# Relative-position attention on one core: halved relative-value products, a picks buffer per query tile, and the band moved in two trimmed transfers

## The chip, the cores and the metric

The kernel runs on one core of a Trainium2 chip. The metric is the device time of one execution in microseconds; the time before is the median of three runs. The core's engines are named as the profile names them: PE (TensorE, its weight loads apart as PEld), DVE (VectorE), ACT (ScalarE), POOL (GpSimd), and SP, which in this kernel only issues transfers and waits.

## What is computed

A two-layer network on 16 sequences of 256 tokens with 128 features. Layer 0 is a second-order linear attention and a top-2 mixture of small experts; layer 1 is an attention with relative positions beside a top-2 mixture of gated experts. The change lies in the attention of layer 1 alone:

```python
# b = 16, s = 256, H = 16 heads of hd = 8, R = 64, VOCAB = 2R + 1
dist = jnp.clip(idx[None, :] - idx[:, None], -R, R) + R
pe_k = rel_emb_k[dist]
pe_v = rel_emb_v[dist]
score = jnp.einsum('bhqd,bhkd->bhqk', q, k) + jnp.einsum('bhqd,qkd->bhqk', q, pe_k)
attn = jax.nn.softmax(score, axis=-1)
ctx = jnp.einsum('bhqk,bhkd->bhqd', attn, v) + jnp.einsum('bhqk,qkd->bhqd', attn, pe_v)
return ctx @ W_out + b_out
```

Here `q`, `k` and `v` come from one projection of the normalized input. The relative part of the scores depends on the distance, which is clipped at 64 on both sides, and so does the relative part of the values.

## The kernel before

The stage `attn1_stage` goes through 16 sequences, each in two query tiles of 128 rows (`it` 0 and 1), so 32 tiles (`s`). In a tile the 16 heads go in eight pairs (`hp` 0 to 7), called slots below. Every engine has its own instruction list, written by hand; waits on semaphores tie them together.

**PE**, in each slot: `key_scores` (L1416) for the pair, `rel_scores` (L1407) of the same pair for the next tile, `transposes` (L1426) of the attention two pairs back. For the tile before it has, spread over the slots, four groups of `rel_values` (L1451, slots 2 to 5), four groups of `weigh` (L1463, value products, slots 3 to 6) and `folds` (L1471, slot 7). The projection of queries and keys of a later sequence (`project_qk`, L1225) stands in slot 1 of tile 1, that of the values (`project_v`, L1400) in slot 7 of tile 0. Both write the PSUM tile `a1ps_p`, which is also the second buffer of `rel_values`.

**Relative values.** The transposed attention of 16 query rows times a table of relative values gives, for each row, all shifted sums; `pick_diagonal` on DVE (L1618) multiplies by a mask that keeps those of the row's own shift, and `folds` sums them up. A group of 16 rows (`ig`) that reaches both key tiles takes two tables, one for each half of the array's columns. A group that reaches only one key tile has one table; the other half of the columns is fed with a table of zeros. Of the four groups of a tile two are of that kind:

```python
if len(use) == 1:
    use.append((len(TABLES), use[0][1]))
```

**The band.** The relative scores of a tile are 192 numbers per query and head (`BAND`) that have to be shifted by one column per row. ACT copies them from PSUM to `a1Rt` (`keep_R`, L1542). SP sends them to a buffer in memory, `skew` (`send_band`, L1741), and fetches them back with a row pitch that is one short (`fetch_band`, L1750) into `a1Sb`, which DVE adds to the scores (`add_scores`, L1609). Each tile's band goes in four quarters `q`, two head pairs each: four sends and four fetches of 384 KB. ACT may write a quarter of `a1Rt` again when the fetch of the tile before has landed.

**SP's list** sets the order of all transfers (`step` of the sync block). It is, for tile 0 of a sequence, with the query stacks of the next sequence (`a1stk<-parts`, L1268, three transfers per `fill`):

```python
fill(0); send_band(s + 1, nit, 0); fetch_band(s, it, 3)
fill(1); send_band(s + 1, nit, 1); fetch_band(s + 1, nit, 0)
fill(2); send_band(s + 1, nit, 2); fetch_band(s + 1, nit, 1)
send_band(s + 1, nit, 3); fetch_band(s + 1, nit, 2)
```

For tile 1 `fill(0)` issues the key stack (L1278), the other two fills are empty, and `send_parts` (L1259), which writes the split queries and keys of the sequence after next to memory, stands after `fetch_band(s + 1, nit, 1)`. A fetch waits for its send to have landed, a send for ACT's copies, and `fill(0)` of tile 0 for the `parts` that were sent in the tile before.

**Start.** DVE clears `a1vx` (L1680) and the edges of `a1Sb` (L1681, L1682); SP's first send and POOL wait for that.

## Time and profile before

| | us |
|---|---|
| median of three runs (lowest, highest) | 1687.14 (1685.96, 1688.66) |
| span of the profiled execution | 1677.5 |
| what lies around the span (median less span) | 9.6 |
| PE busy | 1552.2 (93%) |
| DVE busy | 904.4 (54%) |
| ACT busy | 732.4 (44%) |
| POOL busy | 299.0 (18%) |

The profile is one execution, from its first to its last instruction. The profiled execution has no time of its own other than its span; the runs were timed without the profiler. Busy shares are averages over stages: layer 0 takes up to about 830 us, the experts of layer 1 to about 1100, and the stage of the change about 1102 to 1660. A stretch of the trace therefore says more than the page's first lines. Matmuls are pipelined, so what one costs is read from the start of the next, not from its own duration.

### The profile page before, as it was taken

To read this page: it belongs to the slowest core of one execution; us is meant where nothing else is said; L and a number is where in the kernel's file an instruction comes from. 1 tells how busy PE (TensorE), PEld (TensorE's weight loads), DVE (VectorE), ACT (ScalarE), POOL (GpSimd) and SP (SyncE) were. 2 spreads that over 40 slices of the span, in tenths; PEclk is the share of its full clock that TensorE was granted. 3 is DMA by queue.
4 is the path that set the end of the run, shared out by engine and by line. 5 is a ranking of instruction groups with operands and counts; after the bars stand their busy time and mean duration, and the time that the engine had idled before them with its cause. 6 is when DMAs were issued, how large, how long until landed. Compare 5 with 4: busy or idle time off the path is not lost. (4 is left out here: it accounts for less than half of the span.)

```text
span 1677.5 us, 38807 instructions
## 1 busy us (share of the span) xinstructions
PE 1552.2 (93%) x14424; PEld 1233.4 (74%) x14424; DVE 904.4 (54%) x3193; ACT 732.4 (44%) x1975; POOL 299.0 (18%) x376
## 2 busy tenths in 40 slices
PE   6899999999999999999599999959999999999996
PEld 5668888888888888888365656537777777777764
DVE  5336545454545454545322222237877777777774
ACT  2322222222222222222223232258888888888873
POOL 2010201111111101010430000003323332333232
PEclk9999999999999999999699999979999999999998
DMA  4009400000000000000243232258889998899886
GB/s 118 0 8 86 105 8 7 8 8 6 6 6 5 7 5 7 3 10 4 85 114 114 77 112 85 72 166 245 250 241 251 237 250 235 246 246 254 236 235 173
DMA packets 234032, 181.50 MB, mean 108 GB/s; under 512 B 82703, under 2 KB 223913, under 8 KB 233888
## 3 DMA queue, kind: packets, MB, share of 16 engines
q1 hardware_dynamic: 228514, 167.17, 37.1%
q0 software_dynamic: 5376, 12.44, 2.7%
q8 instruction: 89, 1.46, 0.4%
q14 instruction: 53, 0.43, 0.1%
HBM read 103.63 MB, written 75.78 MB: 107 GB/s over the span
## 5 line engine op out<-in xcount | busy, mean ns | idle before, releaser
L1547 ACT ACTIVATE a1Pm<-a1Pm,a1nmx 128x256 f32<-128x256 f32 x512 | 255.5, 504 | 0.4 <-DVE a1nmx L1609 0.3
L1609 DVE CUSTOM_DVE_ANT_0 a1Pm<-a1ps_S,a1Sb 128x256 f32<-128x256 f32 x512 | 196.1, 421 | 77.2 <-issue 75.5
L768 DVE TENSOR_TENSOR a0AT<-a0ps_AM,mask 128x384 f32<-128x384 f32 x256 | 125.5, 551 | 192.5 <-PE a0ps_AM L588 192.1
L773 DVE TENSOR_TENSOR a0MT<-a0ps_AM,mask 128x384 f32<-128x384 f32 x256 | 138.4, 555 | 88.2 <-PE a0ps_AM L609 85.1
L1542 ACT ACTIVATE a1Rt<-a1ps_R 128x384 f32<-128x384 f32 x264 | 128.6, 487 | 106.7 <-PE a1ps_R L1407 96.9
L1162 DVE TENSOR_TENSOR f1hid<-f1ge,f1ps_b 128x512 f32<-128x512 f32 x80 | 55.0, 688 | 192.1 <-PE f1ps_b L1095 182.4
L1426 PE MATMUL a1ps_T<-ident,a1Pm 128*128 128x128 f32 x1024 | 155.9, 275 | 0.0
L607 PE MATMUL a0ps_AM<-a0AT 128*128 128x256 f32 x512 | 152.9, 380 | 0.0
L572 PE MATMUL a0ps_qk<-xnT_all,a0w_in 128*128 (+1 forms) x512 | 138.3, 393 | 2.0 <-PEq L151 1.3
L715 ACT ACTIVATE a0qk<-a0ps_qk 128x512 f32<-128x512 f32 x128 | 76.4, 597 | 119.3 <-PE a0ps_qk L572 119.3
L1407 PE MATMUL a1ps_R<-rel_st,a1stk 72*128 72x192 bf16 x528 | 90.0, 253 | 35.5 <-ACT a1Rt L1542 13.2
L719 ACT ACTIVATE a0v<-a0ps_v 128x512 f32<-128x512 f32 x64 | 38.2, 597 | 191.0 <-PE a0ps_v L598 187.0
L1426 PEld LDWEIGHTS a1ps_T<-ident,a1Pm 128*128 128x128 f32 x1024 | 115.0, 142 | 0.4 <-issue 0.2
L723 ACT ACTIVATE a0oT<-a0ps_o 128x512 f32<-128x512 f32 x64 | 38.2, 597 | 170.2 <-PE a0ps_o L621 170.2
L608 PEld LDWEIGHTS a0ps_AM<-a0AT 128*128 128x128 f32 x512 | 97.3, 190 | 13.2
L1105 PE MATMUL f1ps_o<-f1wo,f1hid 128*128 128x128 f32 x768 | 90.0, 277 | 15.4 <-DVE f1hid L1162 15.4
L572 PEld LDWEIGHTS a0ps_qk<-xnT_all,a0w_in 128*128 128x128 f32 x512 | 87.1, 190 | 19.9 <-issue 12.1
L1105 PEld LDWEIGHTS f1ps_o<-f1wo,f1hid 128*128 128x128 f32 x768 | 87.0, 192 | 19.7 <-DVE f1hid L1162 11.9
L1416 PE MATMUL a1ps_S<-a1stk 72*128 72x256 bf16 x512 | 101.4, 280 | 0.0
L1093 PE MATMUL f1ps_a<-f1xT,f1w 128*128 128x512 f32 x192 | 100.0, 603 | 0.7 <-issue 0.7
L1547 ACT ACTIVATION_READ_ACCUMULATOR a1Pm<-a1Pm,a1nmx 128x1 f32 x512 | 99.6, 195 | 0.0
L609 PE MATMUL a0ps_AM<-a0AT 128*128 128x128 f32 x512 | 99.0, 275 | 0.0
(246 smaller groups left out, 2991.0 us busy)
## 6 DMA issues: line engine op xcount, KB each, us to landing
skew<-a1Rt SPq DMA_DIRECT2D x132, 384.0 KB, 5.4
a1Sb<-skew SPq DMA_DIRECT2D x131, 384.0 KB, 7.0
a1stk<-parts SPq DMA_DIRECT2D x153, 64.0 KB
a1stk<-parts SPq DMA_DIRECT2D x51, 192.0 KB
parts<-a1prt SPq DMA_DIRECT2D x18, 384.0 KB
f1w<-in_L_ffn_w_kernel SPq DMA_DIRECT2D x16, 344.0 KB
f1w<-in_L_ffn_w_kernel SPq DMA_DIRECT2D x16, 320.0 KB
f1wo<-in_L_ffn_wo_kernel SPq DMA_DIRECT2D x16, 320.0 KB
```

The source lines that it names most:

```text
L572: ins = nc.tensor.matmul(ps_qk[:, i, :], w_in[:, i, p * P:(p + 1) * P], xnT_all[:, bass.ds(b * T, T)], start=True, stop=True)
L607: nc.tensor.matmul(M[:, 0:T], S[:, 0:P], S[:, 0:T], start=True, stop=True)
L609: nc.tensor.matmul(M[:, T:HB], S[:, T:HB], S[:, T:HB], start=False, stop=True).then_inc(M_done, 1)
L768: nc.vector.tensor_tensor(AT[i][h][:, :], ps_AM[i][h][:, 0:HB], mask[:, :], ALU.mult).then_inc(A_ready, 1)
L773: nc.vector.tensor_tensor(MT[i][h][:, :], ps_AM[i][h][:, 0:HB], mask[:, :], ALU.mult).then_inc(M_ready, 1)
L1093: nc.tensor.matmul(ps_a[u % 2][:, :], w[i][:, u * P:(u + 1) * P], xT[i][:, :], start=True, stop=True).then_inc(a_done, 1)
L1105: ins = nc.tensor.matmul(ps_o[i][:, s, :], hid[:, c, s * P:(s + 1) * P], wo[i][:, c, :], start=(c == 0), stop=(c == HC - 1))
L1416: ins = nc.tensor.matmul(ps_S[hp % 2][:, n, :], stk[par][:, 0, h, it * P:(it + 1) * P], stk[par][:, 1, h, :], start=True, stop=True)
L1426: ins = nc.tensor.transpose(ps_T[k % 2][:, n, jt, :], Pm[:, place(2 * k + n), jt * P:(jt + 1) * P], ident[:, :])
L1542: nc.scalar.activation(Rt[:, hp, :, :], ps_R[:, :, :].rearrange("p n c -> p c n"), ACT.Copy).then_inc(sm["R_ready"], 1)
L1547: nc.scalar.activation(Pm[:, place(h), :], Pm[:, place(h), :], ACT.Exp, bias=nmx[it][:, h:h + 1], scale=-1.0, accum_out=den[it][:, h:h + 1 ...
L1609: nc.vector.tensor_tensor_reduce(out=Pm[:, place(h), :], in0=ps_S[hp % 2][:, n, :], in1=bias_of(it, hp, n), scale=-1.0, scalar=3.0e38, op0 ...
```

## The change

It has six parts.

1. A group of `rel_values` with one table no longer multiplies by zeros: its two 8-row halves go to the two halves of the array's columns, four products instead of eight. Groups are taken in the order `turns`: a two-table group, the two one-table groups, the other two-table group.
2. `pick_diagonal` follows that: for a one-table group two instructions, each on 64 partitions and half the columns. What they leave unwritten must be zero, so the picks have a buffer per query tile, `X[0]` and `X[1]`, which DVE clears at the start. The wait for the folds goes one tile further back.
3. The groups of `weigh` stand in slots 3, 4, 6, 6 instead of 3, 4, 5, 6.
4. `project_qk` and ACT's `keep_qk` stand in slot 1 of tile 0 instead of tile 1, with waits to match.
5. Each `send_band` and `fetch_band` is two transfers of 64 rows, one of them 128 columns wide and the other 192 (`halves`), and `a1Sb` has a region for each query tile. Semaphores of the band count 32 instead of 16.
6. ACT waits for the send of the band, not for its fetch, before it writes `a1Rt` again.

```diff
-        Sb = m.sb("a1Sb", [P, HP, 2 * REL + BAND, 2])
+        Sb = m.sb("a1Sb", [P, HP, T + BAND, 2])
-        X = m.sb("a1X", [P, H1, P])
+        X = [m.sb(f"a1X{i}", [P, H1, P]) for i in range(2)]
...
+        def turns(it):
+            one_tile = [k for k in range(4) if alone(it, k)]
+            two_tiles = [k for k in range(4) if not alone(it, k)]
+            return two_tiles[0], *one_tile, two_tiles[1]
...
                 def project_qk(n):
-                    pe.wait_ge(sm["v_ready"], up(n - 1))
-                    pe.wait_ge(sm["X_ready"], up((n - 2) * 8))
+                    pe.wait_ge(sm["v_ready"], up(n - 2))
+                    pe.wait_ge(sm["X_ready"], up(((n - 2) * 2 - 1) * 4))
...
-                        if len(use) == 1:
-                            use.append((len(TABLES), use[0][1]))
                         for w in range(2):
-                            at = ig * GI + w * GH1
-                            for half, (t, jt) in enumerate(use):
-                                c = (1 - w) * (P // 2)
+                            at, c = ig * GI + w * GH1, (1 - w) * (P // 2)
+                            uses = uses_of(it, ig)
+                            pieces = [(w, n, *uses[0])] if alone(it, k) else [(half, 2 * n + w, *use) for half, use in enumerate(uses)]
+                            for half, col, t, jt in pieces:
...
-                        if it == 1 and hp == 1:
+                        if it == 0 and hp == 1:
                             project_qk(r * 2 + par + 2)
...
-                            if 3 <= hp < 7:
-                                weigh(s - 1, prev_b, pit, hp - 3)
+                            for q, at in enumerate((3, 4, 6, 6)):
+                                if hp == at:
+                                    weigh(s - 1, prev_b, pit, q)
...
-                        act.wait_ge(skew_in[hp // PQ], s * 16)
+                        act.wait_ge(skew_out[hp // PQ], s * 32)
...
+                    if alone(it, k):
+                        for w in range(2):
+                            rows = slice(w * (P // 2), (w + 1) * (P // 2))
+                            ins = nc.vector.tensor_tensor(out[rows, w:4:2, :, :], got[rows, 0:2, :, :],
+                                                          bc(bc(pick[rows, :], 1, H1), 1, 2), ALU.mult)
...
-                nc.vector.memset(Sb[:, :, 0:REL, :], 0.0)
-                nc.vector.memset(Sb[:, :, REL + BAND:2 * REL + BAND, :], 0.0).then_inc(sm["cleared"], 1)
+                for i in range(2):
+                    nc.vector.memset(X[i][:, :, :], 0.0)
+                nc.vector.memset(Sb[:, :, P:P + BAND, :], 0.0).then_inc(sm["cleared"], 1)
...
+                def halves(it):
+                    near, far = slice(0, P // 2), slice(P // 2, P)
+                    return ((near, P // 2, P), (far, 0, BAND)) if it == 0 else ((near, 0, BAND), (far, 0, P))
...
                 def send_band(s, it, q):
-                    c0 = 0 if it == 0 else 2 * (P - 1)
-                    sp.dma_start(skew[it][:, ps, c0:c0 + 2 * BAND], Rt[:, ps, :, :].rearrange("p n c h -> p n (c h)")).then_inc(skew_out[q], 16)
+                    for rows, c, w in halves(it):
+                        to = 2 * (c + (0 if it == 0 else P - 1))
+                        sp.dma_start(skew[it][rows, ps, to:to + 2 * w], Rt[rows, ps, c:c + w, :].rearrange("p n c h -> p n (c h)")).then_inc(skew_out[q], 16)
...
                 def fetch_band(s, it, q):
-                    sp.wait_ge(skew_out[q], (s + 1) * 16)
+                    sp.wait_ge(skew_out[q], (s + 1) * 32)
...
+                    for rows, _, w in halves(it):
...
+                        sp.dma_start(Sb[rows, ps, to:to + w, :].rearrange("p n c h -> p n (c h)"),
+                                     bass.AP(flat.tensor, at, [[2 * (HP * PITCH - 1), P // 2], [2 * PITCH, PQ], [1, 2 * w]])).then_inc(skew_in[q], 16)
```

Three places show how the instructions move. On PE, tile 1 of the first sequence, from the third group of `rel_values` to the end of slot 6, before (`a1ps_X` and `a1ps_p` are the two buffers of that group, `a1ps_c` takes the value products, `a1ps_S`, `a1ps_R` and `a1ps_T` are the scores, relative scores and transposes of a slot):

```order
1319 L1451 MATMUL a1ps_X<-a1PT,tabs 64x128 x8
1320 L1463 MATMUL a1ps_c<-a1PT,a1vx 32x128 x8
1321 L1416 MATMUL a1ps_S<-a1stk 128x256 x2
1322 L1407 MATMUL a1ps_R<-rel_st,a1stk 128x192 x2
1323 L1426 MATMUL a1ps_T<-ident,a1Pm 128x128 x4
1324 L1451 MATMUL a1ps_p<-a1PT,tabs 64x128 x8
1325 L1463 MATMUL a1ps_c<-a1PT,a1vx 32x128 x8
1326 L1416 MATMUL a1ps_S<-a1stk 128x256 x2
1327 L1407 MATMUL a1ps_R<-rel_st,a1stk 128x192 x2
1328 L1426 MATMUL a1ps_T<-ident,a1Pm 128x128 x4
1329 L1463 MATMUL a1ps_c<-a1PT,a1vx 32x128 x8
```

The same slots in the changed kernel:

```order
1319 L1463 MATMUL a1ps_X<-a1PT,tabs 64x128 x4
1320 L1475 MATMUL a1ps_c<-a1PT,a1vx 32x128 x8
1321 L1430 MATMUL a1ps_S<-a1stk 128x256 x2
1322 L1421 MATMUL a1ps_R<-rel_st,a1stk 128x192 x2
1323 L1440 MATMUL a1ps_T<-ident,a1Pm 128x128 x4
1324 L1463 MATMUL a1ps_p<-a1PT,tabs 64x128 x8
1325 L1430 MATMUL a1ps_S<-a1stk 128x256 x2
1326 L1421 MATMUL a1ps_R<-rel_st,a1stk 128x192 x2
1327 L1440 MATMUL a1ps_T<-ident,a1Pm 128x128 x4
1328 L1475 MATMUL a1ps_c<-a1PT,a1vx 32x128 x16
```

The third group has four products instead of eight, and the value products of slot 5 have gone to slot 6, where there are now 16.

On SP, tile 0 of a sequence, from the first query stack to the third send, before (L1741 sends a quarter of the band, L1750 fetches one):

```order
159 L1268 DMA a1stk<-parts 8x16x256 x3
160 L1741 DMA skew<-a1Rt 128x2x384
161 L1750 DMA a1Sb<-skew 128x2x384
162 L1268 DMA a1stk<-parts 8x16x256 x3
163 L1741 DMA skew<-a1Rt 128x2x384
164 L1750 DMA a1Sb<-skew 128x2x384
165 L1268 DMA a1stk<-parts 8x16x256 x3
166 L1741 DMA skew<-a1Rt 128x2x384
```

The changed kernel at the second stack and what follows it (L1770 sends, L1783 fetches):

```order
176 L1268 DMA a1stk<-parts 8x16x256 x3
177 L1770 DMA skew<-a1Rt 64x2x384
178 L1770 DMA skew<-a1Rt 64x2x256
179 L1783 DMA a1Sb<-skew 64x2x384
180 L1783 DMA a1Sb<-skew 64x2x256
181 L1770 DMA skew<-a1Rt 64x2x384
182 L1770 DMA skew<-a1Rt 64x2x256
183 L1783 DMA a1Sb<-skew 64x2x384
184 L1783 DMA a1Sb<-skew 64x2x256
185 L1278 DMA a1stk<-parts 24x16x256 x3
```

The order of quarters and stacks is the same; each band transfer is two instructions, of 64 rows each.

On DVE, at the start of the stage, before (the last row belongs to the first slot):

```order
562 L1680 MEMSET a1vx 128x2048
563 L1681 MEMSET a1Sb 128x8x128
564 L1682 MEMSET a1Sb 128x8x128
565 L1606 MEMSET a1taker 1x1
566 L1609 ISA a1Pm,a1nmx<-a1ps_S,a1Sb 128x256
```

And in the changed kernel:

```order
562 L1701 MEMSET a1vx 128x2048
563 L1703 MEMSET a1X 128x2048 x2
564 L1704 MEMSET a1Sb 128x8x384
565 L1619 MEMSET a1taker 1x1
566 L1622 ISA a1Pm,a1nmx<-a1ps_S,a1Sb 128x256
```

Two clears of 2048 elements have come in, and that of the band is 3072 elements in one piece.

## Rows read from the trace of the kernel before

**Rows 1.** Windows, steady part: length, busy us (instructions) by engine, clock, DMA share, GB/s.

```profile
1250.00:1600.00 350.00, 334.69 (x4836) 262.83 (x4830) 269.10 (x1205) 289.79 (x959) 106.15 (x144) 1.00 0.89 244
```

**Rows 2.** Timeline of PE, one sequence: start, us, instruction, records, idle before and releaser.

```profile
1315.38 0.34 PE L1407 MATMUL a1ps_R<-rel_st,a1stk 72*128 72x192 bf16 x2 [0.67 <-ACT a1PT L1558]
...
1316.20 1.09 PE L1451 MATMUL a1ps_X<-a1PT,tabs 128*64 128x128 f32 x16
1317.23 0.39 PE L1416 MATMUL a1ps_S<-a1stk 72*128 72x256 bf16 x2
...
1331.43 1.13 PE L1225 MATMUL a1ps_p<-xnT_all,a1w_in 128*128 128x256 f32 x4 [0.59 <-DVE a1vx L1594]
```

**Rows 3.** Waits, 1108 to 1655 us: who, for whom, us in total, times, longest.

```profile
ACT a1Rt L1542 <- PE a1ps_R L1407: 87.5, 107, 2.8
...
PE a1ps_R L1407 <- DMA a1stk<-parts: 6.4, 6, 2.0
PE a1ps_p L1225 <- DVE a1vx L1594: 6.1, 10, 0.7
```

**Rows 4.** Timeline of SP, one round from first query stack to the next.

```profile
1315.23 2.08 SPq L1268 DMA_DIRECT2D a1stk<-parts  x3
1317.36 0.45 SPq L1741 DMA_DIRECT2D skew<-a1Rt  x1
...
1321.18 0.47 SPq L1750 DMA_DIRECT2D a1Sb<-skew  x1
...
1324.35 0.46 SPq L1741 DMA_DIRECT2D skew<-a1Rt  x1
...
1329.90 0.36 SPq L1750 DMA_DIRECT2D a1Sb<-skew  x1
1330.30 1.38 SPq L1278 DMA_DIRECT2D a1stk<-parts  x3
1331.87 0.38 SPq L1741 DMA_DIRECT2D skew<-a1Rt  x1
...
1340.22 0.36 SPq L1750 DMA_DIRECT2D a1Sb<-skew  x1
...
1344.02 1.53 SPq L1259 DMA_DIRECT2D parts<-a1prt  x1
...
1348.21 1.38 SPq L1268 DMA_DIRECT2D a1stk<-parts  x2
```

**Rows 5.** Timeline of SP: the first query stack of the first and the last round.

```profile
1113.00 2.10 SPq L1268 DMA_DIRECT2D a1stk<-parts  x3
...
1620.89 2.08 SPq L1268 DMA_DIRECT2D a1stk<-parts  x3
```

**Rows 6.** Lines, 1108 to 1655 us: one of the picks; count, busy us, mean ns, idle before.

```profile
L1618 DVE TENSOR_TENSOR a1X<-a1ps_p,pick 128x512 f32<-128x512 f32 x62 | 42.5, 686 | 0.0
```

**Rows 7.** Timeline of DVE, start of the stage: clearing, and the first slot.

```profile
1102.58 1.76 DVE L1680 MEMSET a1vx<- 128x2048 f32 x1 [13.05 <-PEq L1031]
...
1115.69 0.06 DVE L1606 MEMSET a1taker<- 1x1 f32 x1 [9.20 <-DMA a1Sb<-skew]
```

**Rows 8.** Timeline of SP, start of the stage: the first four sends and three fetches.

```profile
1106.52 4.75 SPq L1741 DMA_DIRECT2D skew<-a1Rt  x4
1111.31 1.65 SPq L1750 DMA_DIRECT2D a1Sb<-skew  x3
```

**Rows 9.** The page's sixth part: band transfers, KB each, median us to landing.

```profile
skew<-a1Rt SPq DMA_DIRECT2D x132, 384.0 KB, 5.4
a1Sb<-skew SPq DMA_DIRECT2D x131, 384.0 KB, 7.0
```

More of the change, by code:

```diff
@@ L1376, in bias_of, with uses_of, alone @@
         def bias_of(it, hp, n):
-            c0 = REL * (1 - it)
+            c0 = BAND * it
             return Sb[:, hp, c0:c0 + T, n]
+        def uses_of(it, ig):
+            return [(t, jt) for t, (i2, jt, g2) in enumerate(TABLES) if (i2, g2) == (it, ig)]
+        def alone(it, k):
+            return len(uses_of(it, 2 * k)) == 1
+        def turns(it):
+            one_tile = [k for k in range(4) if alone(it, k)]
+            two_tiles = [k for k in range(4) if not alone(it, k)]
+            return two_tiles[0], *one_tile, two_tiles[1]
         def tiles_behind(r, i):
@@ L1427, in transposes, with rel_values @@
                     ins.then_inc(sm["T_done"], 1)
-                def rel_values(s, b, it, k):
-                    pe.wait_ge(sm["X_ready"], up(s * 4 + k - 1))
-                    if k == 1:
+                def rel_values(s, b, it, j):
+                    k, to = turns(it)[j], ps_X[j % 2]
+                    pe.wait_ge(sm["X_ready"], up(s * 4 + j - 1))
+                    if j == 1:
                         pe.wait_ge(sm["v_ready"], b + 1)
-                        pe.wait_ge(sm["qk_ready"], b + 3)
-                    if k == 0:
+                        pe.wait_ge(sm["qk_ready"], min(b + (3 if it == 0 else 4), B + 2))
+                    if j == 0:
                         pe.wait_ge(sm["Ta_ready"], (s + 1) * 4)
@@ L1464, in weigh, with folds @@
                                              start=(q == 0 and part == 0), stop=False)
-                def folds(s):
+                def folds(s, it):
                     pe.wait_ge(sm["X_ready"], (s + 1) * 4)
@@ L1531, in _ @@
                     weigh(last, B - 1, 1, q)
-                folds(last)
+                folds(last, 1)
                 project_out(last)
@@ L1574, in step @@
                             keep_rdT(s - 1)
-                        if it == 1 and hp == 1:
+                        if it == 0 and hp == 1:
                             keep_qk(nc, act, front, ps_p, bias_q, bias_k, r * 2 + par + 2)
@@ L1611, in add_scores, with pick_diagonal @@
                                                        accum_out=nmx[it][:, h:h + 1]).then_inc(sm["S_ready"], 1)
-                def pick_diagonal(s, k):
-                    v.wait_ge(sm["X_done"], s * 4 + k + 1)
-                    v.wait_ge(sm["c_done"], s)
-                    out = X[:, :, k * 2 * GI:(k + 1) * 2 * GI].rearrange("p h (n i) -> p n h i", n=4)
-                    nc.vector.tensor_tensor(out, ps_X[k % 2], bc(bc(pick[:, :], 1, H1), 1, 4), ALU.mult).then_inc(sm["X_ready"], 1)
+                def pick_diagonal(s, it, j):
+                    k, got = turns(it)[j], ps_X[j % 2]
+                    v.wait_ge(sm["X_done"], s * 4 + j + 1)
+                    v.wait_ge(sm["c_done"], up(s - 1))
+                    out = X[it][:, :, k * 2 * GI:(k + 1) * 2 * GI].rearrange("p h (m i) -> p m h i", m=4)
+                    if alone(it, k):
[3 more added lines that the diff above has]
+                                                          bc(bc(pick[rows, :], 1, H1), 1, 2), ALU.mult)
+                    else:
+                        ins = nc.vector.tensor_tensor(out, got, bc(bc(pick[:, :], 1, H1), 1, 4), ALU.mult)
+                    ins.then_inc(sm["X_ready"], 1)
                 def divide(s):
@@ L1689, in _ @@
                 for k in range(4):
-                    pick_diagonal(last, k)
+                    pick_diagonal(last, 1, k)
                 combine(last - 1)
@@ L1795, in _ @@
                 for q in range(QUARTERS - 1):
[L1796 to L1797 removed]
+                    sp.wait_ge(skew_in[q], (2 * B + 1) * 32)
+                sp.wait_ge(skew_out[3], (2 * B + 1) * 32)
 def store_stage(nc, x_all, out):
```

21 lines of the change are left out of this document (9 added, 12 removed).

## The prediction

> **What bounds the kernel now.** I began with the page's forty slices, took from them the stretch of the second attention (about 1102 to 1660 us), and put its steady part into one window [rows 1]. There PE is busy 334.69 of 350 us (96%), ACT 83%, DVE 77%, the DMA engines 0.89, and the granted clock is 1.00 throughout (2.4 GHz). So matmul work taken out of this stage should come out of the time, unless something that is nearly as late takes over. The timeline of PE [rows 2] shows how small its holes are: two of 0.6 us in a batch element. The waits of the whole stage [rows 3] say who makes them: the value bias on DVE (the query projection shares a PSUM tile with it), and the query stacks, a DMA that SP issues. ACT by contrast waits 87.5 us for PE in 107 places, so it has room.
>
> The second thing to see is SP's own order [rows 4]. One batch element (two query tiles) is one round of SP: three query stacks with sends and fetches of the band between them, the key stack, more sends and fetches, then `parts` for the element after next, and the next round's first stack may not go before these parts have landed. The round is therefore a closed loop of issues and landings: 1315.23 to 1348.21 is 32.98 us. From the first to the last first-stack [rows 5] there are 15 rounds in 507.89 us, 33.86 each. That PE does wait for the query stacks, 6.4 us in six places, says that this loop arrives just in time with PE at 96%: **two bounds of nearly the same length**. What PE saves counts only as far as SP's round shortens too.
>
> **The change part by part.** *Halved products.* A group of 16 records (8 products) starts at 1316.20 and the next matmul at 1317.23: 1.03 us [rows 2]. Of four groups per tile two lose half: 1.03 us less per tile, 33 us over 32 tiles, 2.06 us per element, all of it on PE. Records still alternate between the column halves, so I take half the number as half the time. If the two halves no longer overlapped, nothing would be saved (0); there is no way to save more than half. I take the half, since a group with two tables already alternates in the same way at that rate.
>
> *The moved query projection.* In tile 0 the PSUM tile is free, so the wait of 0.59 us goes [rows 2] (6.1 us in ten places over the stage [rows 3]). The ACT wait of 0.67 us that PE has in the tile without a projection turns up in tile 1 instead. About 0.4 us per element is gained. *The moved value products* (3, 4, 6, 6) are the same instructions in the slots that the picks left emptier; nothing.
>
> *Picks.* One pick is 686 ns [rows 6]. Two half-length ones cost between 0.69 and 1.37 us together; at the upper end DVE gets 1.4 us more per tile. DVE is at 77%, and a pick is not used before the folds of slot 7, so this is hidden. It would cost if DVE fell behind PE by a slot; it has 0.77 x 16.9 = 13.0 us of work per tile, 14.4 after. *Two pick buffers* take away a wait that no row shows; nothing.
>
> *ACT's wait on the send instead of the fetch* frees the band tile sooner. What ACT waits for is PE, in 107 places [rows 3], so nothing is gained in the steady part.
>
> *Start of the stage.* DVE clears 2048 elements in 1.76 us from 1102.58, and the first band send leaves SP at 1106.52 when it is done with all clearing [rows 7, 8]. The change clears twice 2048 more and 3072 instead of 2048: 3 x 1.76 + 2.64 + gaps of 0.16 puts the end at about 1111.0. The four sends so far waited for ACT's copies and were out at 1111.3; now eight go from 1111.1 at about 0.42 us each, to 1114.4. The first fetch, issued at 1111.31 and waited for until 1115.69, comes 3.1 us later and its second half 0.4 more: **+3.5 us**, bare, since DVE is idle 9.2 us there. Bounds: 0 if the copies still set the pace, 4.5 if all of it shows.
>
> *The halved transfers.* Every send and fetch of 384 KB [rows 9] becomes one of 128 KB and one of 192 KB: a sixth fewer bytes, twice the issues. An issue holds SP 0.36 to 0.47 us [rows 4]; 16 more per element are 6 to 7 us of SP. Not all lies on the loop. I walk the round of [rows 4] with 0 at 1315.23:
> - To the third send, 9.12 us, is pure issuing. Four second halves before it: 10.9.
> - That send's landing releases the fetch at 14.67, 5.55 later. If the queue ahead decides, it lands at 14.67 as before; if the issue decides, at 10.9 + 0.45 + 5.55 = 16.9. The queue ahead is as long in packets and shorter in bytes. I take 15.4.
> - The key stack follows 0.85 later instead of 0.40: 16.25 (was 15.07).
> - From the keys to the landing of the next send it is 9.92 us (24.99), most of it the keys' own transfer; the second half hides under it. Half of the sixth that the bands lose, 8%, comes off: 25.4.
> - From there to `parts` it was 3.80 us, with waits for ACT and for a send that ACT had released late. These are over by then, and three issues with their halves remain: 2.6, so 28.0 (was 28.79).
> - The parts landed 4.19 later; less 8%: **31.9 instead of 32.98, -1.0 us per round.**
>
> Low bound: nothing of the second halves shows and the landings shrink by the full sixth; the round is then shorter than PE's own and PE sets it, 33.86 - 2.06 - 0.4 = 31.4, or -2.4. High bound: the issue decides and no landing shrinks: 16.9, keys 17.75, 27.7, 30.3, 34.5, or +1.5. I take -1.0 because at a DMA share of 0.89 a landing is mostly queue, and the queue is what shrinks.
>
> For the halves the trace of before has no example. A rule speaks against them: the Trainium skill, page DMA: Bandwidth & Descriptors, section Rules for kernel authors, says of two transfers to disjoint partition halves "Don't bother — they serialize", and wants one transfer over all partitions. By it alone the sum would keep the issues and lose the shrinking, which is the high bound above; by the bytes of the rows it is the -1.0. No run so far shows which.
>
> **The sum.** 15 rounds x -1.0 = -15.0; start +3.5; the last two tiles, after the last stack, are PE's and SP has nothing left to do in them, -2.0. Together -13.5 us. The profiled span is 1677.5 us and the median of the runs 1687.14, 9.6 more around the span, which the change doesn't touch: 1664 in the profile, **1674 us** by the runs.
>
> **The rivals.**
> - *PE sets the pace alone.* For it: 96% busy, waits for the stacks only 6.4 us in total. Against: with 2.4 us less per element the loop would have to come down from 33.9 to 31.4 with 16 more issues in it. 15 x -2.4 + 3.5 - 2 = -34.5: 1653 us.
> - *SP's issues set the pace.* The second half of each transfer holds the stacks behind it; the round goes to 34.5, PE waits for the query stacks at the start of every second tile, and what the products save turns into that wait. This decides from the point where the third send lands more than about 1.2 us later than now. 15 x 1.5 + 3.5 - 2 = +24: 1711 us; half-way there, +0.7 per round, 1699. For it: the pure issuing up to the third send. This is where the rule of the Trainium skill cited above would lead.
> - *Nothing in the end.* Rounds at -0.1 to -0.3 pay for the start: 1684 to 1690 us.
> - *The products don't overlap.* If the halves of the array took turns instead of working side by side, PE would keep its time and the rounds theirs; this falls together with the case before.
>
> **How the numbers follow.** The sum's case, rounds shorter by 0.3 to 2.0 us (1665 to 1684), gets 0.45; PE alone (1650 to 1665) 0.22; nothing 0.13; SP's issues (1691 to 1711) 0.20. What a measurement of this kernel can tell from no change is about 0.2%, 3.4 us. So faster 0.67, same 0.13, slower 0.20. The range leaves out the lower tip of the second case and the upper half of the last: 1652 to 1700 us.
>
> **What would show it.** Right: the rounds between first stacks come to 32.9 us on average; PE's busy time falls by about 33 us and its share in the steady window to 93 or 94%; PE's wait for the query stacks grows from 6.4 to 15 or 20 us; the landing of the key-phase send comes 9 us after the keys; DVE's first pass waits about 3.5 us longer. If the rounds are 31.4 and the waits for stacks are gone, PE was the only bound and I gave the loop too much weight. If they are 34 or more, with issues back to back on SP and PE waiting 2 us or more for the stacks in each element, the second halves lay on the loop. If the groups of 8 records last 1 us, the products didn't overlap. A landing that is longer than before at fewer bytes would be against every case here.

## The result and the profile after

The changed kernel takes **1713.57 us** (median of four runs, 1711.48 to 1717.45), the kernel before 1686.55 beside it: ratio 1.0174, 95% interval 1.0148 to 1.0201. It is slower by 27 us (forecast: 1674, range to 1700). The profiled execution is the slowest of the four and spans 1715.7 us.

The steady window, as in [rows 1] (length; PE, PEld, DVE, ACT and POOL busy; clock; DMA share; GB/s):

```profile
1250.00:1600.00 350.00, 310.55 (x4267) 242.46 (x4261) 265.92 (x1172) 274.78 (x907) 98.50 (x135) 0.96 0.79 201
```

Every engine does less in the same 350 us, and the DMA engines are down from 0.89 to 0.79. Nothing that the window counts as busy looks like the bound. What it does not count is SP's issuing. Timeline of SP, one round, the counterpart of [rows 4] (at 37.78 us the longest of 15; their mean is 35.64):

```profile
1371.27 2.13 SPq L1268 DMA_DIRECT2D a1stk<-parts  x3
1373.44 1.46 SPq L1770 DMA_DIRECT2D skew<-a1Rt  x2
1374.95 1.27 SPq L1783 DMA_DIRECT2D a1Sb<-skew  x2
1376.26 2.12 SPq L1268 DMA_DIRECT2D a1stk<-parts  x3
1378.42 1.27 SPq L1770 DMA_DIRECT2D skew<-a1Rt  x2
1379.73 2.25 SPq L1783 DMA_DIRECT2D a1Sb<-skew  x2
1382.03 2.12 SPq L1268 DMA_DIRECT2D a1stk<-parts  x3
1384.19 1.27 SPq L1770 DMA_DIRECT2D skew<-a1Rt  x2
1385.50 1.27 SPq L1783 DMA_DIRECT2D a1Sb<-skew  x2
1386.81 1.26 SPq L1770 DMA_DIRECT2D skew<-a1Rt  x2
1388.12 1.28 SPq L1783 DMA_DIRECT2D a1Sb<-skew  x2
1389.44 1.52 SPq L1278 DMA_DIRECT2D a1stk<-parts  x3
...
1394.58 1.27 SPq L1770 DMA_DIRECT2D skew<-a1Rt  x2
1401.08 1.24 SPq L1783 DMA_DIRECT2D a1Sb<-skew  x2
...
1405.05 0.53 SPq L1259 DMA_DIRECT2D parts<-a1prt  x1
...
1409.05 2.12 SPq L1268 DMA_DIRECT2D a1stk<-parts  x3
```

From 1371.27 to 1391 each row begins where the one above it ended: tile 0 of the list has become pure issuing. One real wait is left, 5.2 us from 1395.85 to 1401.08, for the landing of a send. Over 15 rounds SP issues for 30.5 us of 35.6 on average; in the kernel before it was 16.0 of 33.9. A pair of halves holds SP for 1.27 us, where one transfer of 128 rows took 0.36 to 0.47 [rows 4]. Band lines of both kernels (ns, minimum/median/maximum), first after, then before:

```profile
L1770 SPq DMA_DIRECT2D skew<-a1Rt x264: 589/612/1737, 1113.4 to 1691.6; - x132
L1783 SPq DMA_DIRECT2D a1Sb<-skew x262: 592/609/1926, 1118.7 to 1692.9; - x131
```

```profile
L1741 SPq DMA_DIRECT2D skew<-a1Rt x132: 359/382/1487, 1106.5 to 1651.6; - x132
L1750 SPq DMA_DIRECT2D a1Sb<-skew x131: 359/366/1732, 1111.3 to 1652.0; - x131
```

A transfer of 64 rows costs *more* to issue than one of 128 rows, at its minimum (0.59 against 0.36 us) as at its median. A round has eight sends and eight fetches by quarter, so SP issues 16 x (1.22 - 0.37) = 13.6 us more in a round of 34. Waits from 1108 to 1700 us, first the engines (as [rows 3]), then SP's own queue, after and before (before: 1108 to 1655 us; who, for whom, us, times, longest):

```profile
DVE a1taker L1619 <- DMA a1Sb<-skew: 38.4, 29, 9.5
PE a1ps_R L1421 <- DMA a1stk<-parts: 35.2, 15, 3.8
```

```profile
SPq L1783 <- DMA skew<-a1Rt: 58.3, 25, 5.2
SPq L1770 <- ACT a1Rt L1555: 13.8, 27, 1.2
```

```profile
SPq L1750 <- DMA skew<-a1Rt: 119.6, 69, 6.3
SPq L1741 <- ACT a1Rt L1542: 103.1, 66, 3.8
```

PE waits 2.3 us for the query stacks in each of 15 elements (35.2 us; 6.4 before [rows 3]), and SP waits for a third of what it did: in the kernel before 119.6 us for sends to land and 103.1 for ACT, now 58.3 and 13.8. The first share in the list of the chain that ended last is `SPq 13%` (before, `PE 21%`).

The transfers themselves did become shorter, as the sixth part of the profile's page has it (KB each, median us to landing; before, 5.4 and 7.0 [rows 9]):

```profile
skew<-a1Rt SPq DMA_DIRECT2D x132, 192.0 KB, 3.6
a1Sb<-skew SPq DMA_DIRECT2D x131, 192.0 KB, 4.2
skew<-a1Rt SPq DMA_DIRECT2D x132, 128.0 KB, 3.7
a1Sb<-skew SPq DMA_DIRECT2D x131, 128.0 KB, 4.6
```

And the start of the stage, DVE and then SP, as in [rows 7, 8]:

```profile
1104.09 1.76 DVE L1701 MEMSET a1vx<- 128x2048 f32 x1 [13.06 <-PEq L1031]
...
1110.72 2.62 DVE L1704 MEMSET a1Sb<- 128x3072 f32 x1 [0.59 <-issue]
1122.86 0.06 DVE L1619 MEMSET a1taker<- 1x1 f32 x1 [9.52 <-DMA a1Sb<-skew]
```

```profile
1113.37 5.29 SPq L1770 DMA_DIRECT2D skew<-a1Rt  x8
1118.71 3.88 SPq L1783 DMA_DIRECT2D a1Sb<-skew  x6
```

From the first clearing to the first slot it is 18.8 us, 13.1 before: +5.7.

### The profile page after: what moved, and what is told of

Read it like the earlier page. It is cut to its first block and busy times, and to the rows that moved or that the text cites. A ratio compares the mean times of both kernels' runs of the same rounds, so it can differ in the third digit from the quotient of the medians.

```text
span 1715.7 us, 38103 instructions
## 1 busy us (share of the span) xinstructions
PE 1544.1 (90%) x13904; PEld 1225.4 (71%) x13912; DVE 927.5 (54%) x3258; ACT 733.0 (43%) x1975; POOL 298.9 (17%) x376
## 5 line engine op out<-in xcount | busy, mean ns | idle before, releaser
L1440 PE MATMUL a1ps_T<-ident,a1Pm 128*128 128x128 f32 x1024 | 169.1, 291 | 0.3 <-ACT a1Pm L1560 0.3
L1421 PE MATMUL a1ps_R<-rel_st,a1stk 72*128 72x192 bf16 x528 | 94.9, 265 | 62.1 <-DMA a1stk<-parts 35.2
L1440 PEld LDWEIGHTS a1ps_T<-ident,a1Pm 128*128 128x128 f32 x1024 | 125.5, 152 | 1.1 <-ACT a1Pm L1560 0.6
L1421 PEld LDWEIGHTS a1ps_R<-rel_st,a1stk 72*128 72x128 bf16 x528 | 46.7, 102 | 90.1 <-DMA a1stk<-parts 39.4
L1430 PE MATMUL a1ps_S<-a1stk 72*128 72x256 bf16 x512 | 106.5, 292 | 4.0 <-DVE a1nmx L1622 4.0
```

The source lines that it names most:

```text
L1421: ins = nc.tensor.matmul(ps_R[:, n, :], stk[par][:, 0, 2 * hp + n, it * P:(it + 1) * P], rel_st[:, it, :], start=True, stop=True)
L1430: ins = nc.tensor.matmul(ps_S[hp % 2][:, n, :], stk[par][:, 0, h, it * P:(it + 1) * P], stk[par][:, 1, h, :], start=True, stop=True)
L1440: ins = nc.tensor.transpose(ps_T[k % 2][:, n, jt, :], Pm[:, place(2 * k + n), jt * P:(jt + 1) * P], ident[:, :])
```

## The experiments

The round below is the mean distance of POOL's copies of `a1xb`, one per element, between the second and the last (15 intervals); by this measure before has 33.64 us and the changed kernel 35.56. Ratios are to the kernel before, run on the same chip beside each group. "Move" is the query projection in tile 1 or tile 0; "parts" is where SP sends them. "Half" products come with the other parts of the change that the columns don't name (picks, slots of `weigh`, ACT's wait on the send). Not in the columns: e5, e7, e11, e12 and e16 clear the edges of the band first. The groups ran on different chips, so between groups the ratios compare better than the times, and each round is that of one profiled execution.

| run | products | transfers | move | parts | us | ratio (95%) | round |
|---|---|---|---|---|---|---|---|
| before | full | whole | tile 1 | late | 1686.55 | 1 | 33.64 |
| after | half | trimmed halves | tile 0 | late | 1713.57 | 1.0174 (1.0148, 1.0201) | 35.56 |
| e1_one_transfer | half | whole | tile 0 | late | 1685.78 | 1.0013 (0.9996, 1.0029) | 33.67 |
| e2_halves_alone | full | trimmed halves | tile 1 | late | 1716.64 | 1.0205 (1.0180, 1.0230) | 35.68 |
| e3_wide_halves | half | wide halves | tile 0 | late | 1737.02 | 1.0313 (1.0289, 1.0338) | 37.25 |
| e4_by_head_pair | half | 128 rows, one pair | tile 0 | late | 1700.88 | 1.0100 (1.0078, 1.0123) | 35.00 |
| e5_one_transfer_early | half | whole | tile 0 | late | 1681.96 | 1.0000 (0.9972, 1.0028) | 33.67 |
| e6_stacks_from_pool | half | trimmed halves | tile 0 | late | 1695.31 | 1.0071 (1.0049, 1.0093) | 34.24 |
| e7_early_parts | half | whole | tile 0 | early | 1684.93 | 1.0023 (1.0007, 1.0038) | 33.94 |
| e8_before_early_parts | full | whole | tile 1 | early | 1674.56 | 0.9962 (0.9947, 0.9977) | 33.51 |
| e9_sends_from_act | half | trimmed, sends by ACT | tile 0 | late | 1693.19 | 1.0072 (1.0045, 1.0100) | 34.50 |
| e10_sends_act_early_parts | half | trimmed, sends by ACT | tile 0 | early | 1694.72 | 1.0080 (1.0051, 1.0110) | 34.73 |
| e11_split_behind_copy | half | whole | tile 0, split later | early | 1655.50 | 0.9843 (0.9802, 0.9883) | 32.31 |
| e12_project_back | half | whole | tile 1 | early | **1649.15** | 0.9815 (0.9774, 0.9857) | 31.83 |
| e13_project_early_alone | full | whole | tile 0 | late | 1710.28 | 1.0158 (1.0113, 1.0204) | 35.77 |
| e14_after_project_back | half | trimmed halves | tile 1 | late | 1708.19 | 1.0154 (1.0134, 1.0175) | 35.46 |
| e15_after_split_behind_copy | half | trimmed halves | tile 0, split later | late | 1710.20 | 1.0177 (1.0157, 1.0197) | 34.74 |
| e16_project_back_late_parts | half | whole | tile 1 | late | 1676.51 | 0.9965 (0.9946, 0.9984) | 33.72 |
| e17_trim_off_sp | half | trimmed, sends by ACT | tile 1 | early | 1671.72 | 0.9950 (0.9932, 0.9968) | 33.08 |

**What the transfers cost.** Four runs: the changed kernel with whole transfers, the kernel before with halves alone, and two other ways to cut a transfer in two.

e1: `send_band` and `fetch_band` as before, all else changed.

```diff
-                    for rows, c, w in halves(it):
-                        sp.dma_start(skew[it][rows, ps, to:to + 2 * w], Rt[rows, ps, c:c + w, :]...)
+                    sp.dma_start(skew[it][:, ps, c0:c0 + 2 * BAND], Rt[:, ps, :, :]...)
```

> The changed kernel with its transfers undone: one transfer of 128 rows and 192 columns per band quarter, as before, and everything else as changed. Theory A (the issues of the halves on SP make the round long: 0.61 us each, so 1.3 us per quarter instead of 0.42): the round from first query stack to first query stack falls from 35.6 us to between 31.4 and 33, PE's wait for the stacks to 10 us or less, the time to 1650 to 1675 us. Theory B (the reordered PE work, the picks in two steps or the moved projection lengthen the round): the round stays at 34 us or more and the time at 1700 us or more. Theory C (no single part; the stage was limited by transfers all along): the time comes back to about that of before, 1687 us.

e2: the reverse, the halves put into the kernel before.

> The kernel before with the halved, trimmed transfers alone (its band tile with a region for each query tile, its clearing to match); products, picks, slots and projection as before. Theory A: SP's round has the same list as in the changed kernel, so it is again 35 to 36 us, and the time is 1705 to 1715 us, although PE has all its old work. Theory B: about 1687 us. Theory C: below 1687 us, since a sixth of the band's bytes is gone.

e3: halves by rows, but both of the full 192 columns.

```diff
+                    for rows in (slice(0, P // 2), slice(P // 2, P)):
+                        sp.dma_start(skew[it][rows, ps, c0:c0 + 2 * BAND], Rt[rows, ps, :, :]...)
```

> The changed kernel with the halves of 64 rows but both 192 columns wide, so as many issues as changed and as many bytes as before (band tile laid out as before). Theory A: issues at 0.6 us as in the changed kernel, round 35.5 to 37 us, time 1712 to 1735 us; what it lies above the changed kernel is what the trimming is worth, at most 1 us per round. If the bytes decide rather than the issues, the round grows by 2 us or more.

e4: two transfers of all 128 rows, one head pair each, full width.

```diff
+                    for h in range(q * PQ, (q + 1) * PQ):
+                        sp.dma_start(skew[it][:, h:h + 1, c0:c0 + 2 * BAND], Rt[:, h:h + 1, :, :]...)
```

> The changed kernel with two transfers per band quarter that are split by head pair instead of by rows: 128 rows, one head pair, 192 columns each. As many issues and as many bytes as in the run with wide halves, but all 128 rows in each. If an issue of 64 rows is dear because of its rows, these go at 0.36 to 0.42 us, the round is 32.5 to 34.5 us and the time 1670 to 1695 us. If an issue costs 0.6 us whenever a quarter is cut, round and time are those of the wide halves.

The halves alone cost the kernel before 2.05% (e2), as much as the whole change; without them (e1) the slowdown is gone. So **the halved transfers make the slowdown by themselves**. (In e2 ACT still waits for the fetch before it writes `a1Rt` again, 30.9 us in 14 places, so not all of e2's loss need be SP's.) The wide halves (e3) are 23 us worse than the trimmed ones, 1.7 us per round: fewer bytes are worth that much in a kernel of this kind, more than I had allowed, and less than the second issue costs. In e4 an issue of a send takes 0.44 us at the median, in e3 0.61:

```profile
L1765 SPq DMA_DIRECT2D skew<-a1Rt x264: 319/435/2077, 1111.9 to 1677.6; - x132
```

The time of e4 lies between: 17 us above before, with the same number of transfers as e3 and the same bytes. The shape of a transfer, then, and not its size sets what it costs SP. e3 and e4 differ in the shape alone, and lie 36 us (2.1%), 2.25 us per round, apart. Not all of that need be the issue: the wide halves also land later (medians 5.0 and 5.2 us against 4.1 and 3.1), and no run separates the two.

Not all expectations held. e1 came out at the time of theory C; e2 and e3 lie just above theory A's times; e4 missed its 1670 to 1695, and its issue its 0.36 to 0.42.

The surprise is e1: two of the four groups of a tile have lost half of their products, and the time is that of before. That was the open question of all that follows.

**Where SP stood.** e5 is e1 with the edges of the band cleared first, so that the first sends start sooner. e6 is the changed kernel with the nine query stacks issued by POOL at the start of tile 0.

```diff
+                    if it == 0:
+                        pool.wait_ge(sm["R_ready"], (r * 4 + i + 1) * HP)
+                        stack_queries(nc.gpsimd, front, parts, r * 2 + par + 1, 1 - par, into=front.pool_in)
```

> As the run with one transfer per quarter, and DVE clears the edges of the band tile first, so that SP's first send no longer waits for the clearing of the other buffers. The first slot of DVE starts about 13 us after DVE's first clear with the order of before and about 5 us later with two pick buffers cleared first; with the band first it starts 8 to 11 us after it. So 3 to 8 us less than the run with one transfer per quarter and, by theory A, 1645 to 1670 us, below both kernels.

> The changed kernel with its halved, trimmed transfers, but the nine query stacks of a sequence are issued by POOL, at the start of tile 0, instead of by SP: about 6.3 us of issuing less on SP per round, no transfer less. Theory A: SP is the limit through its issues, so the round falls by 3 us or more, to 31.4 to 33 us, and the time to 1650 to 1680 us. If the transfers themselves (the engines that move them) set the round, it stays at 35 us and the time at 1705 to 1720 us. POOL may be too slow in issuing; then PE's wait for the query stacks grows and the time is above 1713 us.

Both missed theory A. e5 is at 1.0000 beside 1.0013 for e1: an earlier start is worth 2 us by the ratios, 4 by the medians, and both lie within the intervals. Taking the stacks off SP (e6) returns 18 of the 27 us, but not the rest.

e7 and e8 shorten the loop through SP where it closes: the parts go out earlier in tile 1, in e7 on top of e5, in e8 in the kernel before.

```diff
+                    if it == 1:
+                        ...
+                        send_parts(sp, front, parts, r * 2 + par + 2)
                     send_band(s + 1, nit, 2)
                     fetch_band(s + 1, nit, 1)
-                    if it == 1:
-                        ...
-                        send_parts(sp, front, parts, r * 2 + par + 2)
```

> The kernel e5_one_transfer_early (halved products, whole 128-row transfers, round 33.9 us, 1682 us), with the sending of the split parts moved, in the second tile of a batch, from behind the third fetch of the band to ahead of the third send: some 7 us earlier on SP. Its landing is what the next round's query stacks wait for (before: 14.1 us in 5 waits, 2.8 each). Theory L, the round is the loop through SP (stacks, bands, parts, stacks again): the wait goes, a round takes 31.4 to 32.5 us, and 15 rounds give 1646 to 1661 us; PE's busy share rises to 96% or more. Theory C, the round is the chain of the compute engines or the landing of the bands: the stacks come earlier and wait elsewhere, the round stays at 33.5 to 34 and the time at 1675 to 1686.

> The kernel before with the same move of the parts alone, its products of full size. Theory L with PE as the second bound: the round falls only as far as PE's busy time lets it (334.69 of 350 us, so 32.4 of 33.86): 32.4 to 33.3 us, 1662 to 1679 us in all. Theory C: 33.7 to 34 and 1680 to 1688. The difference of e7_early_parts to this run is what the halved products are worth once the loop is shorter: 10 to 25 us by theory L, nothing by theory C.

e9 and e10 move the sends of the changed kernel to ACT's queue; SP keeps the waits that stood ahead of them.

```diff
                         exponentials(s, it, hp)
+                        if hp % PQ == PQ - 1:
+                            send_band(s + 1, 1 - it, hp // PQ)
```

> The changed kernel, with the two halves of every send issued by ScalarE behind its own evictions; SP keeps the waits at the places of the sends, so the order of its other work is the same. It takes 16 issues of 0.61 us, 9.8 us, off SP's round and puts them on ScalarE, which was busy 98.5 of 350 us. Theory I, the slowdown is SP's issue time alone: the round returns to 33.0 to 34.0 us and the time to 1672 to 1692. Rival, the smaller transfers are slower by themselves, or the chain of the first tile stays late for another reason: 35 us or more per round and 1700 or more.

> e9_sends_from_act with the parts sent early as in e7_early_parts. Theories I and L together: 31.2 to 33 us per round, 1640 to 1670 in all, since both waits of SP's loop are gone and the trimmed transfers land sooner. Theory C: as e9_sends_from_act, 1672 to 1692.

e8 gains 6.4 us and e7 nothing: the loop through SP is not all that holds the kernel with the halved products back. e9 gains 20 us on the changed kernel (17 by the ratios) and stays at 1.0072; e10 the same. Theory L failed for e7 and e10 and held for e8's time only, not for its round (33.51); e9 lies between its two cases. (The expectation of e9 takes 98.5 of 350 us for ACT's busy time; that is POOL's, and ACT's is 274.78.) The waits of e7 (1108 to 1700 us) show why. PE no longer waits for the query stacks; it waits for DVE, once in each element and in one place, the transposing of the reciprocals (PEld and PE record the same gaps):

```profile
PEld a1ps_c L1491 <- DVE a1rrep L1668: 30.0, 17, 1.9
PE a1ps_c L1491 <- DVE x_all L1650: 26.5, 16, 1.7
```

e6 and e9 have the same wait (PE 28.5 and 23.2 us, 16 times each), so what they did not give back meets the same obstacle.

**The copy beside GpSimd's split.** In that place DVE copies the reciprocals, `a1rrep`, 128x128 from SBUF to SBUF. In the kernel before all 32 copies take 0.23 us; in e7 16 of 32 take 0.8 to 1.12 us, all those of tile 1. The move of the query projection to tile 0 is what brought POOL's split of its result (five instructions of 1.04 to 1.17 us) forward to the start of tile 1. Three runs test it: e11 makes POOL wait until the copy is done, e12 puts the projection back, e13 moves the projection alone in the kernel before.

```diff
+                        pool.wait_ge(sm["rrep_ready"], r * 4 + i)
                         split_qk(nc.gpsimd, pool, front, one, r * 2 + par + 2, ...)
```

> e7_early_parts (1685 us) with one wait more: GpSimd begins to split the projections only when VectorE has copied a1rrep. In e7 that copy took 1.11 us in the second tile of 15 of the 16 batches and ended with GpSimd's first splitting instruction beside it (1403.71 to 1404.84, the copy 1403.74 to 1404.85); in before it took 0.23 us every time. TensorE waited for it and for the addition behind it (55 us in 31 waits), and its granted clock fell to 0.5 in the three us after that gap. Theory P, the collision of the copy with GpSimd gives the halved products' gain back: every copy takes 0.23 us, 0.9 us per round comes back from the wait and 0.5 to 1.5 from the clock, so a round takes 31.5 to 33.0 us and the whole 1643 to 1672. Rival, the gap is VectorE's other work there and closes by nothing else: at most 0.5 us per round, 1677 to 1686.

```diff
-                        if it == 0 and hp == 1:
+                        if it == 1 and hp == 1:
                             project_qk(r * 2 + par + 2)
```

> e7_early_parts with the projection of the next batch (and its eviction) put back from the first tile to the second, with the waits of before: what is left of the change is the halved products, the picks buffer per tile, the other slots and the single trimmed skew check, on whole transfers. GpSimd's split starts later, behind a1rrep, and the projection's four matmuls fill the gap in which TensorE waited for VectorE. Theory P: copies of 0.23 us, TensorE's clock at 0.98 or more, 1643 to 1672. Rival, the loop is bound by something that all variants share: 1675 to 1686 again.

> The kernel before with the move of the projection alone (second tile to first, its waits changed with it), products, transfers and buffers as before. Theory P: 12 or more of the 16 copies of a1rrep in second tiles take 0.5 to 1.2 us, TensorE waits for them 0.9 us or more per round, and the time rises by 10 to 35 us, to 1692 to 1717. Rival, the copy's 0.9 us are hidden behind TensorE, which has more to do here: within 5 us of before, 1677 to 1687, with slow copies all the same.

(The "skew check" in the expectation of e12 is ACT's wait on the send instead of the fetch.)

All three came out as the collision has it: 1655.5, 1649.15 and 1710.28, with 32 copies of 0.23 us in e11 and e12 and 16 slow ones in e13. **The move alone costs 27 us** (1.0158). e11 is e7 with one wait more and nothing else, so it is the collision that costs, and not the other place of the projection. The place in e13, DVE, POOL and PE (start, us, instruction, idle before and releaser):

```profile
1384.11 1.11 DVE L1647 COPY a1rrep<-a1rden 128x128 f32<-128x128 f32 x1
...
1385.74 0.27 DVE L1629 TENSOR_TENSOR x_all<-x_all,a1ps_c 128x128 f32<-128x128 f32 x1
```

```profile
1384.08 1.05 POOL L1246 TENSOR_TENSOR a1prt<-a1qkf,one 128x512 bf16<-128x512 f32 x1
```

```profile
1386.16 0.45 PE L1479 MATMUL a1ps_c<-ident,a1rrep 128*128 128x128 f32 x1 [1.72 <-DVE x_all L1629]
1386.53 1.98 PE L1451 MATMUL a1ps_X<-a1PT,tabs 128*64 128x128 f32 x16
```

POOL's instruction starts at 1384.08 and ends at 1385.13; the copy starts 0.03 us later and ends at 1385.22. It lasts as long as its neighbour runs. The same two instructions in the kernel before, DVE and POOL, lie 2.3 us apart:

```profile
1400.78 0.23 DVE L1647 COPY a1rrep<-a1rden 128x128 f32<-128x128 f32 x1
```

```profile
1403.26 1.04 POOL L1246 TENSOR_TENSOR a1prt<-a1qkf,one 128x512 bf16<-128x512 f32 x1 [3.50 <-ACT a1qkf L1235]
```

The Trainium skill states this as a rule (page SBUF — State Buffer, section SBUF: two separate sides): DVE in its two-port modes and GpSimd share one port pair, an exclusive lock for a whole instruction, and the later one blocks. The trace agrees in the main: 0.23 us alone, 1.11 behind an instruction of 1.05. But the copy ends 0.09 us behind its neighbour, less than the 0.23 that it takes alone, and no run here shows why.

The 0.9 us are not the whole price. Windows of 1 us in e13 (columns as above):

```profile
1383.00:1384.00 1.00, 0.35 (x4) 0.35 (x5) 1.00 (x8) 1.00 (x3) 0.89 (x1) 1.00 0.84 250
1384.00:1385.00 1.00, 0.43 (x4) 0.20 (x2) 0.97 (x2) 1.00 (x5) 0.98 (x2) 1.00 0.98 248
1385.00:1386.00 1.00, 0.00 (x0) 0.00 (x0) 1.00 (x5) 0.07 (x1) 0.92 (x2) 1.00 1.11 230
1386.00:1387.00 1.00, 0.84 (x5) 0.65 (x7) 0.71 (x6) 0.60 (x3) 0.92 (x2) 0.56 1.11 184
1387.00:1388.00 1.00, 1.00 (x14) 1.00 (x12) 0.00 (x0) 1.00 (x4) 0.92 (x2) 0.50 1.17 208
1388.00:1389.00 1.00, 1.00 (x9) 0.54 (x6) 0.00 (x0) 0.13 (x1) 0.92 (x2) 0.50 0.90 178
1389.00:1390.00 1.00, 1.00 (x9) 0.83 (x8) 0.79 (x6) 0.60 (x2) 0.83 (x1) 0.73 0.80 272
```

PE is busy 0.35, 0.43 and 0.00 in three windows, DVE 1.00; then the granted clock is 0.50 (1.2 of 2.4 GHz) for about three us, and the group of 16 records at 1386.53 takes 1.98 us instead of 1.09 [rows 2]. Over [rows 1]'s window the clock is 0.96 in e13 and 1.00 in e12. Not each gap of PE does it: e12 has one with 0.63, 0.00 and 0.19 (1382 to 1385) and the clock stays at 1.00 behind it. From e7 to e11 PE's wait in this place falls from 26.5 to 11.4 us, 15 of the 29 us gained, and the clock of the window rises from 0.95 to 0.99. That the other half is the clock fits these rows; no run shows it by itself. (The 55 us in the expectation of e11 count PEld and PE, the same gaps twice.)

**How the causes combine.** e14 and e15 mend the second cause in the changed kernel, by putting the projection back and by the wait; e16 is e12 with the parts sent late; e17 is e12 with the trimmed halves, the sends issued by ACT, and the start's clearing as in the changed kernel.

> The changed kernel with the projection put back in the second tile, halved transfers kept. Theory S, the halves hold the round by themselves: SP's list of issues (two of 0.61 us in each quarter) sets a round of 35 to 36 us as in e2_halves_alone, whatever the compute engines save: 1700 to 1716, little or nothing below the changed kernel. Rival, additive: e2's 33 us and the 34 us that the halved products gave in e12_project_back cancel: 1676 to 1690.

> The changed kernel with GpSimd's split behind the copy of a1rrep, the one wait of e11_split_behind_copy. 12 of 16 copies there took 0.3 to 1.2 us, 6.9 us in all. Theory S: the copies take 0.23 us and the time stays at 1700 to 1716, since SP's list sets the round. Rival, additive: 1678 to 1692.

> e12_project_back with the parts sent where before sends them, behind the third fetch: so the halved products, picks and slots on whole transfers, nothing else moved. If the early parts add nothing to them, 1645 to 1656 as e12; if the loop through SP is near, as the 7 us that they gave before say, 1656 to 1672, with TensorE or SP waiting for the query stacks.

> e12_project_back (1649 us) with the trimmed halves of the changed kernel again, but with the sends issued by ScalarE as in e9, SP issuing only the fetches in halves. It tells whether fewer bytes would pay where SP's issue time does not stand against them. If they do: rounds below those of e12, 1630 to 1646. If the compute engines now set the round and ScalarE's own issues are in its way, 1650 to 1670, above e12, and the trimming is worth nothing to this kernel.

e14 and e15 bring next to nothing (1.0154 and 1.0177 against 1.0174), although 13 of 16 copies are slow in the changed kernel and none in these two: as long as SP issues all the halves, its list and the landing it waits for hold the round. (By the round e15 looks 0.8 us better than after, but its profiled execution was the lowest of its four runs, that of after the highest; the medians differ by 3.4 us.) e16 missed its expectation, which was 1645 to 1672: 1676.5. Halved products (with the picks, slots, ACT's wait and the order of clearing that go with them) give 5 us without the early parts, early parts alone 6.4 (e8), both together 34 (e12; 31 by the ratio). So the 34 us, which the expectation of e14 puts down to the halved products, need both. The waits of e16, 1108 to 1700 us, name the other bound:

```profile
PE a1ps_R L1421 <- DMA a1stk<-parts: 23.1, 15, 2.5
```

In e12, PE's share of the steady window is 331.85 of 350 us at a clock of 1.00, in rounds of 31.83, and PE's wait for the stacks is down to 8.5 us: PE comes nearest to setting the pace there. The DMA engines move 260 GB/s.

```profile
1250.00:1600.00 350.00, 331.85 (x4735) 260.96 (x4734) 293.27 (x1321) 308.47 (x1012) 115.26 (x154) 1.00 0.92 260
```

e17 is 23 us slower than e12, a little above its expectation, so trimming in this form is worth nothing to the fastest version: an issue takes ACT 0.62 us as well, ACT's copies start late by 43.2 us in 65 places (3.6 us in 2 in e12), and the chain that ended last begins with `ACT 17%`. The later clearing is in these 23 us too. Other issuing engines and shapes were not tried. From e10 e17 differs by the projection's place alone, which takes 1.0080 to 0.9950: the second cause once more, in a third kernel. **e12 beats both kernels**, by 1.85% against the kernel before (0.9774 to 0.9857).

## Why the prediction was wrong, point by point

- **Two bounds of nearly the same length** was right, and the runs show it better than the trace did: 5, 6.4 and 34 us in e16, e8 and e12. So was the conclusion that PE's saving counts only as far as SP's round shortens.
- **The issue of a half** is the step that failed. I took 0.36 to 0.47 us for each half from [rows 4]; it measured 0.61. With it "6 to 7 us of SP" per element became 13.6. The walk's four legs against their means over 15 rounds:

| leg of the round | before, mean | walk | measured |
|---|---|---|---|
| first stack to keys | 15.27 | 16.25 | 17.99 |
| keys to the second fetch behind them | 9.80 | 9.15 | 9.45 |
| that fetch to `parts` | 3.13 | 2.6 | 4.25 |
| `parts` to the next first stack | 5.66 | 3.9 | 3.95 |
| round | 33.86 | 31.9 | 35.64 |

  The two legs that wait for a landing came within 0.3 us of the walk; the two that only issue make 3.4 of the 3.7 us that it was short. From the start to the keys SP waits for nearly nothing. The rows held the issue price of another shape only, 128 rows; I bounded the landing from both sides and not the price of the issue.
- **The landings** shrank, by more than the 8% that I took: medians 3.6 to 4.6 us against 5.4 and 7.0 [rows 9]. "A landing that is longer than before at fewer bytes" did not occur. Not all of it is the trimming: in e1, with whole transfers, the fetch's median is 4.9. e3 puts trimming at 1.7 us per round. The case for -1.0 us was right about the landings and lost by the issues.
- **The rival** "SP's issues set the pace", 1711 us at +1.5 us per round, is what happened: 1713.57 at +1.8 (first stacks, [rows 5] against 1122.63 and 1657.28: 35.64). Its sign was named: rounds of 34 or more, issues back to back, PE waiting 2 us or more for the stacks (2.3). I gave it 0.20; and the Trainium skill's rule (page DMA: Bandwidth & Descriptors, section Rules for kernel authors) led there. For its reason, that both halves serialize, no run speaks: the landings fell. What the runs show is the issue time. That its number lies so near is partly luck: its +1.5 was an issue of 0.45 us with landings that did not shrink, and it came about by a dearer issue and shorter landings.
- **The moved query projection** was taken as a gain of 0.4 us per element and is a loss of 2.1 (e13: 35.77 against 33.64). What was missed is that it decides when POOL begins to split, which I did not follow past PE and ACT. Besides, the projection's 1.13 us [rows 2] stood where PE would else wait for DVE at the start of tile 1, so part of it was cover, not load: with the collision gone, PE in e11 still waits there, 11.4 us in 14 places, and in e12 0.8 in one. What that is worth in time is not shown; e11 and e12 lie 6 us apart, and their intervals overlap. In the changed kernel this loss does not show, since SP is later still (e14, e15); it shows as soon as the halves are gone (e1 at 1.0013 against e16 at 0.9965, which also clears the band first).
- **Halved products**: they do overlap; the size was a little off. In e12, two groups:

```profile
1324.43 1.09 PE L1463 MATMUL a1ps_X<-a1PT,tabs 128*64 128x128 f32 x16
1326.38 0.66 PE L1463 MATMUL a1ps_p<-a1PT,tabs 128*64 128x128 f32 x8
```

  Eight records take 0.66 us against 1.09 for sixteen: 0.43 less per group, 0.86 per tile, 27.5 us over 32 tiles (forecast 33). From start to next start it is 0.59 against 1.03, which says the same. PE's total busy time, which was to fall by 33 us, fell by 8.1 (1552.2 to 1544.1), at the clock of 0.96.
- **Picks**: two half picks take 0.42 us each, 0.84 together against 0.686, inside the bounds. **The start** cost 5.7 us, not 3.5: the eight sends took 5.29 us (0.66 each, nearly the same price again) instead of 3.3, and the gaps between the clearings were 0.38 to 0.59 us instead of 0.16.
- **PE alone**, 1653 us with rounds of 31.4, was the case for a kernel in which nothing else is in the way. e12, which leaves out the halved transfers and the move and sends the parts early, is near it: 1649, 31.83.

## What to carry to other kernels

A list of issues is an engine's work like any other: before a transfer is cut in two, price the issue of the new shape, and count what the issuing engine does in the stretch where it never waits. Before an instruction is moved out of a place, look at what waits there: it may be the cover, and what it feeds on a third engine moves with it. Where two bounds stand side by side, test each change in a kernel in which the other bound has been lifted; otherwise a good change reads as nothing.

## What I had not expected of the hardware

A transfer of 64 rows holds its issuing engine 0.61 us (SP; 0.62 on ACT), one of 128 rows and the same columns 0.37 to 0.42 (medians of the kernel before and e1), and one of 128 rows and one head pair instead of two 0.44 to 0.45 (e4): fewer rows cost more, and no run shows why. A DVE copy of 0.23 us that meets a GpSimd instruction takes up to 1.12 us in e7 and 1.24 in e6, and 0.9 us in one place per element, with the clock that falls behind it, were worth 29 us of the whole (e7 against e11).
